# Attention phase: TensorE multiplies weights into an unused bank while it would wait, at the phase's start and in its last pair

## The reference

```python
h = tokens(x)                                  # stem convolution, offsets, deformable convolution: 36 tokens of 192
h = concatenate([h, quantised_embedding(x_txt)], axis=1)          # 36 + 128 = 164 tokens an image
h = h + attention(layernorm(h))                # 12 heads of 16, window of +-64 tokens, softmax, output projection
h = h + kan(layernorm(h))                      # two spline layers, 192 -> 512 -> 192, 16 coefficients an edge
```

```python
q, k, v = (x @ W + b).reshape(B, N, H, d).transpose(0, 2, 1, 3)   # each
scores = where(abs(i - j) <= 64, einsum('bhqd,bhkd->bhqk', q, k) * SCALE, -inf)
out = einsum('bhqk,bhkd->bhqd', softmax(scores), v)
return out.transpose(0, 2, 1, 3).reshape(B, N, D) @ Wo + bo
```

## Time and profile before

| | us |
|---|---|
| median of 3 runs | 2430.45 |
| lowest, highest | 2428.31, 2439.93 |
| profiled execution, span | 2436.7 |
| TensorE multiplying (PE) in it | 2309.0 (95%) |
| VectorE busy (DVE) | 1892.6 (78%) |
| ScalarE busy (ACT) | 1407.7 (58%) |
| GpSimd busy (POOL) | 229.4 (9%) |

### The profile page before, as it was taken

The page is one execution under the profiler, slowest core; times in us unless marked ns, Lnnn a source line. Parts: engine busy times, 40 slices in busy tenths (PEclk is TensorE's granted clock), DMA queues, the critical chain, the costliest instruction groups (busy, mean ns, idle before and its releaser), DMA issues.

```text
span 2436.7 us, 49389 instructions
## 1 busy us (share of the span) xinstructions
PE 2309.0 (95%) x20297; PEld 2155.4 (88%) x20297; DVE 1892.6 (78%) x2364; ACT 1407.7 (58%) x1391; POOL 229.4 (9%) x132
## 2 busy tenths in 40 slices
PE   7699959999999969999999999989999999999999
PEld 6366848888888859999999999989999999999999
DVE  8699745666666668676676766679999999999995
ACT  5588113444444374443534435488888888888881
POOL 5422000000000003121121211000000000000000
PEclk9799967999999969999999999999999999999999
DMA  7655130111111100000000001120000000000000
GB/s 242 164 150 149 55 145 22 44 45 45 44 45 45 45 22 20 26 19 15 26 19 26 19 15 34 64 84 23 23 23 23 23 23 23 23 23 23 23 18 10
DMA packets 99328, 116.26 MB, mean 48 GB/s; under 512 B 15271, under 2 KB 90423, under 8 KB 98487
## 3 DMA queue, kind: packets, MB, share of 16 engines
q1 hardware_dynamic: 79087, 89.38, 12.2%
q10 hardware_dynamic: 16520, 14.75, 2.0%
q0 software_dynamic: 3616, 10.54, 1.7%
HBM read 83.77 MB, written 30.86 MB: 47 GB/s over the span
## 4 chain that ended last, share of the span: by engine, by line
PE 63%; issue 0%; DVE 0%
PE spline_acc L1890 26%; PE spline_acc L1863 10%; PE spline_acc L1862 9%; PE spline_acc L1864 9%; PE spline_acc L1884 5%; PE spline_acc L1886 2%; PE spline_xT L761 0%; DVE spline_f L1639 0%; DVE spline_weights_low L1622 0%; DVE spline_x L1709 0%; DVE spline_x L1712 0%
## 5 line engine op out<-in xcount | busy, mean ns | idle before, releaser
L1890 PE MATMUL spline_acc<-spline_weights,spline_f 128*128 128x192 f32 x3936 | 672.0, 328 | 0.0
L1890 PEld LDWEIGHTS spline_acc<-spline_weights,spline_f 128*128 128x128 f32 x3936 | 637.2, 190 | 0.0
L1863 PE MATMUL spline_acc<-spline_f,spline_weights_high 128*128 128x328 f32 x1536 | 482.7, 314 | 0.0
L1862 PE MATMUL spline_acc<-spline_f,spline_weights_high 128*128 128x328 f32 x1536 | 480.1, 313 | 2.5 <-DVE spline_weights_low L1622 2.5
L1864 PE MATMUL spline_acc<-spline_f,spline_weights_low 128*128 128x328 f32 x1536 | 476.5, 310 | 0.0
L1862 PEld LDWEIGHTS spline_acc<-spline_f,spline_weights_high 128*128 128x128 f32 x1536 | 290.2, 189 | 2.8 <-DVE spline_weights_low L1622 2.8
L1863 PEld LDWEIGHTS spline_acc<-spline_f,spline_weights_high 128*128 128x128 f32 x1536 | 289.3, 188 | 0.0
L1864 PEld LDWEIGHTS spline_acc<-spline_f,spline_weights_low 128*128 128x128 f32 x1536 | 288.9, 188 | 0.0
L1884 PE MATMUL spline_acc<-spline_weights_split,spline_f_high 128*128 128x384 f32 x656 | 218.2, 389 | 8.2 <-issue 8.2
L1639 DVE SCALAR_TENSOR_TENSOR spline_f<-spline_front 128x984 fp32r<-128x984 f32 x128 | 145.5, 1177 | 100.7 <-PE spline_acc L1864 95.0
L1019 DVE TENSOR_REDUCE attend_max<-scores_by_query 82x6 f32<-82x984 f32 x128 | 150.8, 1178 | 67.8 <-PE scores_by_query L1334 67.8
(11 more groups left out here) (224 smaller groups left out, 4286.6 us busy)
## 6 DMA issues: line engine op xcount, KB each, us to landing
spline_front<-pos_scr SPq DMA_DIRECT2D x32, 540.0 KB, 4.4
hid_scr<-spline_hid SPq DMA_DIRECT2D x64, 164.0 KB, 1.8
spline_xn<-hid_scr SPq DMA_DIRECT2D x41, 256.0 KB, 3.1
attend_spread<-rec_scr SPq DMA_DIRECT2D x128, 61.5 KB, 2.2
pix_scr<-spline_front SPq DMA_DIRECT2D x32, 225.0 KB
spline_weights_raw<-w SPq DMA_DIRECT2D x1, 6144.0 KB, 21.3
spline_weights<-w SPq DMA_DIRECT2D x4, 1536.0 KB, 6.3
spline_x<-h_scr SPq DMA_DIRECT2D x41, 96.0 KB, 1.9
```

Of the source, the lines that this page charges most:

```text
L1862: nc.tensor.matmul(z, high, x_high, start=start, stop=False)
L1863: nc.tensor.matmul(z, high, x_low, start=False, stop=False)
L1890: last = nc.tensor.matmul(z, f_rest[i][:, cols], w2[:, i, r, :], start=False, stop=stop)
```

## The change

A helper `keep_going(n, spare)` issues n multiplications of 128 columns of `wqh` (the stationary operand) with the 384 columns of `wkh`, each overwriting `spare`, which nothing reads. The output is `tp`'s first bank where no key scores are pending, and once a bank of `xb` that is claimed for the transposes which follow. It is called with

- 48 at the start of the phase, with the wait for the zeros moved behind it
- 8 between the first transposes and the wait for their being read
- 9 after each of the prelude's four rounds of scores
- 18 in the first pair's first block, ahead of the second quarter's scores
- 20 at the end of `finish`, and 28 after each of the last two output projections

186 multiplications in all, each with its weight load. They carry no semaphore.

```diff
@@ -1264,8 +1264,6 @@
 
         @block.tensor
         def _(pe):
-            pe.wait_ge(zeros_set, 5)
-
             def claim(at):
 
                 bank, c = at
@@ -1277,6 +1275,11 @@
 
                 for bank, c in at:
                     pe.wait_ge(emptied[bank], c + 1)
+
+            def keep_going(n, spare):
+
+                for _ in range(n):
+                    nc.tensor.matmul(spare, wqh[:, 0, 0:P], wkh[:, 0, :], start=True, stop=True)
 
             def turn_x(t, i, at):
                 d, rows = ((0, D0), (D0, D1))[i]
@@ -1402,6 +1405,7 @@
                 for c in range(2):
                     mix(a, u, 1, c, use(t, MIX_LAST[1]))
                 project_out(a - 2, 1, use(t, Y_LAST[1]))
+                keep_going(20, tp[:, 0, 0:HG * P])
 
             def pair(tt, u, first=False, more=True):
                 t = 2 * tt + u
@@ -1419,6 +1423,8 @@
                             keys_scores(a, u, i, q // 2, most, first and i == 0)
                         if q == 0 and i == 1 and more:
                             read(use(t, K_[1]), use(t, K_[2]))
+                        if first and q == 1 and i == 0:
+                            keep_going(18, xb[:, claim(use(t, X[0])), 0:HG * P])
                         if nxt:
                             queries_scores(a + 1, w, 1 - i, q)
                         if q == 0 and not first:
@@ -1452,8 +1458,11 @@
                         for g in range(HG):
                             project(wkh, wkl, g, use(t, K_[g]))
 
+            keep_going(48, tp[:, 0, 0:HG * P])
+            pe.wait_ge(zeros_set, 5)
             for j in range(2):
                 turn_x(0, j, start(START["X"][j]))
+            keep_going(8, tp[:, 0, 0:HG * P])
             read(*(start(START["X"][j]) for j in range(2)))
             for g in range(HG):
                 project(wqh, wql, g, start(START["Q"][g]))
@@ -1464,6 +1473,7 @@
             read(start(START["K"][1]), start(START["K"][2]))
             for q in range(4):
                 queries_scores(0, 0, 0, q, True)
+                keep_going(9, tp[:, 0, 0:HG * P])
             turn_max(0, start(START["MAX"]))
             pe.wait_ge(wo_in, 16)
             pair(0, 0, first=True)
@@ -1475,6 +1485,7 @@
             pair(PAIRS // 2 - 1, 1, more=False)
             for i in range(2):
                 project_out(2 * PAIRS - 2 + i, i, use(PAIRS, Y[i]))
+                keep_going(28, tp[:, 0, 0:HG * P])
 
 
 def spline_phase(nc, front, a, h_scr, hid_scr, out, w_raw, w1_in):
```

## The result

The changed kernel takes 2432.23 us (median of 20 runs), the kernel before 2440.21 (20 runs). The ratio is 0.9969, 95% interval 0.9955 to 0.9983: 7.6 us faster (4.1 to 11.0), a real gain but under the 0.5% at which the prediction split its chances. The forecast was 12.2 us faster, 2418.3 us, in a range of 2412 to 2427; the measured time lies 13.9 us above the one and 5.2 us above the other. Most of that is the base: three runs of the kernel before gave 2430.45, twenty gave 2440.21, which is 9.8 us. The rest is the gain. Single runs of either kernel spread over more than 20 us.

The account below looks back on a forecast made before the run. TensorE, busiest and partly at half clock, was taken to bound the kernel. Start 2.3, rounds 1.0, first block 8.7, second 0.2 and end 0 sum to 12.2 us: 2418.3 us from a 2430.45 median, range 2412 to 2427.

Parts of the forecast that it names:

- What bounds it, and what the low clock costs: TensorE bounds the kernel; an added multiplication costs 0.178 us at the high clock and 0.32 us at the low one.
- The 48: Start of the phase: 11.3 us of multiplications, hidden under the first rows' layer norm; 3.2 us cost if the clock stayed low.
- The prelude: First transposes to first key scores: 2.3 us gained by transposes and projections at the high clock, 1.0 us by the rounds.
- The rounds of 9: Prelude's four score rounds: 2.63 us each with the filling, 0.3 us longer than the wait; 1.0 us gained against those measured.
- The first block: First pair: 19.9 us for 28.7 with the clock high throughout, 8.7 us gained; 1.5 us left empty behind the 18.
- the case that the clock falls there: Rival: clock falls in the first block at the 1.5 us left empty; 5.6 us gained in all, 2424.8 us; chance 0.26.
- The second block: First pair, nothing put in: starts at the high clock and loses it a little later than before; 0.2 us gained.
- the bound of 5.0: Upper bound of the second block's gain, 18.2 - 13.3 us; as a rival that the clock holds there, 2413.5 us, chance 0.13.
- The end: Last pair's 20, 28 and 28: no gain, since the phase ends with VectorE's value chain; bounds +1.5 and -2 us.
- the lower bound: The -2 us bound on the end's effect; a high clock shortens the last projection by some 2 us.
- The base: Kernel before taken at a median of 2430.45 us, three runs with a spread of 11.6, one profiled execution of 2436.7.
- The rule that was set against the change: Clock falls only after one long idle gap, so filling between rounds protects nothing: 1.2 us cost against the start's 2.3.

Follow-up runs that it names:

- hold_front2: The same kernel as hold_front, run once more for a second trace and sample of times: 0.9933 of the kernel before, 2429.68 us.
- hold_pre60: hold_front with 60 multiplications in place of 48 at the start of the phase: 0.9936 of the kernel before, 2431.51 us.
- fill28: The changed kernel with 28 multiplications in place of 18 in the first pair's first block: 0.9952 of the kernel before, 2431.74 us.
- before_look: The kernel before, unchanged, run once more for a second trace: 2430.84 us in one run.
- tail_only: The kernel before with only the 20 and 28 + 28 multiplications at attention's end: 1.0019 of the kernel before, 2449.22 us.
- hold_front: fill28 with 12 more multiplications in the first pair's second block, ahead of its second query scores: 0.9924 of the kernel before, 2421.93 us.
- front_only: The changed kernel without the 20 and 28 + 28 multiplications at attention's end: 0.9979 of the kernel before, 2443.27 us.
- hold_all: hold_pre60 with the waits of the last pair filled by multiplications too: 0.9935 of the kernel before, 2427.88 us.
- hold_thin: hold_all with 6 multiplications in place of 9 in the prelude's four rounds: 0.9915 of the kernel before, 2415.15 us.
- hold_light: hold_front with every added multiplication on 32 rows by 82 columns of weights, not 128 by 128: 1.0018 of the kernel before, 2450.0 us.

## Why the prediction was wrong, point by point

- **What bounds it, and what the low clock costs.** Right. The multiplications cost 0.173 us at the high clock, from start to start (forecast 0.178), and 0.32 at the low one, as forecast.
- **The 48.** Hidden, as forecast. What was missed is what they leave: they end 2.1 us before the transposes, and the clock fell 1.4 us behind these. I had them end 0.9 us before the transposes, by taking 6.1 us for the clock to rise; it rose after 3.5, and the gap grew. hold_front2, where it rose after 5.9 and the gap was 0.95 us, kept the clock.
- **The prelude, 3.3 us forecast, 1.9 measured.** Of the 1.4 us missing 1.0 is this fall: hold_pre60 and hold_front2, without it, give 21.7 us against 24.6, so 2.9. The rest is the rounds.
- **The rounds of 9.** 2.75 us for 2.63 forecast, without a wait and at 1.00, right but for 0.1 us each.
- **The first block, 8.7 us forecast, 2.0 measured.** This is the step that failed: that the clock would hold through this block, over the 1.5 us left empty behind the 18. The size was right and its condition was not: with 28 in place of 18 (fill28) the block is 20.1 us, forecast 19.9 (28.7 - 19.9 is 8.8; the 8.7 of the sum is a slip of 0.1). The hole of 1.5 us behind the 18 was seen and computed (1.49 measured), and the case that the clock falls there was priced at 2.3 us of gain in this block (2.0 measured) but given half the chance of the other. The trace already spoke for it: the clock had been lost beside waits of 1.27 and of 2 us, with the same light work around them. I gave too much weight to the 18 ahead of the hole: 3.4 us of full-size work did not carry the clock over the 1.5 us and the light work behind them, in three traces. The 28.7 us were also taken from one trace. The old start gave 28.7, 24.5 and 28.4 us, 27.2 on the mean, against which the changed kernel's 26.7 is a gain of 0.5.
- **The second block, 0.2 forecast, 0.8 measured**, with the fall where it was expected. The 0.8 can't be put down to the change: before_look and tail_only, with the old start, have 17.5 us too. hold_front bears out the bound of 5.0 (5.3).
- **The end, 0 forecast.** Right by front_only and tail_only, and by the reason given: the last residual follows VectorE's chain. The 2 us of the lower bound exist, but elsewhere. VectorE's norm chain waits for the projection that closes the last pair, and the change's 20 come after it. Here is that wait in the changed kernel, then the same projection in hold_pre60, where it ran at the high clock (2.18 us for 3.86):

```profile
864.00 0.55 DVE L1071 TENSOR_TENSOR attend_h<-attend_spare,attend_resid 82x384 f32<-82x384 f32 x1 [8.44 <-PE attend_spare L1394]
```

```profile
856.08 2.18 PE L1394 MATMUL attend_spare<-attend_wo,attend_oT 128*82 128x192 f32 x12 [0.70 <-ACT attend_mixed L1185]
```

  The stretch behind it is 31.3 us there, and again in hold_all and hold_thin, for 33.1 or more in every trace where it began at the low clock or the clock fell under it.
- **The base.** One profile and three times of the kernel before were taken for it. The three times were 9.8 us below the median of twenty; with the right base the forecast would have been 2428.0 us, 4.2 below the measured one. Its first block alone varies by 4.2 us (before_look) and its last pair by 4.3 (26.8 and 22.5), neither by anything in the code. Of the 7.6 us measured, the start explains 66.8 us against 71.5, 66.8 and 70.7 in three executions with the old start, 2.9 us on the mean. Of these 2.0 are the prelude, the one step that is shorter in every trace (22.7 or 22.8 for 24.6 to 24.9). 2.9 is below the interval's 4.1, and three traces are too few to say where the rest lies.
- **The rule that was set against the change.** The Trainium skill (TensorE: Matmul & The Clock Gate, section "HAM oscillation — how this bites in real kernels") ties a fall to one long idle gap. All three falls of the changed kernel stand beside gaps of 1.49 to 2.11 us, shorter than it names, and filling them removed all three (hold_pre60, fill28, hold_front). The traces disagree with it, as the forecast held; the forecast then let a 1.5 us gap pass. By that rule the prelude would have gained the start's 2.3 us less the rounds' 1.2, so 1.1; it gained 1.9, with a fall in it.

## What to carry to other kernels

Filling TensorE's waits works here as a closed chain: the waits of over 1 us beside light work are filled until dense work of the kernel itself takes over, and one hole of 1.5 us gave back 6.6 us that the fillings ahead of it had prepared. Shorter waits were borne: the pairs from the second to the last but one keep the clock with waits of up to 0.85 us in them, and 0.95 us did no harm in hold_front2. Fill with full-size operands and size each filling just under the wait (6 in place of 9 kept the clock and saved 1.3 us), and read in the trace which projection the end really follows before filling there. Where a kernel's clock is lost and regained, compare step times over several traces: one profile's step may lie 4 us from the next one's. And take the base from as many runs as the result will be measured with: here three runs missed it by more than the change gained.

## What the runs showed of the hardware that was not expected

- 48 multiplications of 32 rows by 82 columns kept TensorE busy for 15.6 us and did not raise the clock; 48 or 60 of 128 by 128 had it up 3.2 to 5.9 us after the first, in ten traces. In this phase being busy was not enough.
- TensorE busy all the time with light work can lose the clock (hold_light, at 365.8) or keep it (its second block).
- The same waits at the same place can lose it in one execution and not in the next: the last pair took 22.5 us in four and 26.1 to 27.1 us in seven of the eleven traces that leave its waits open. A fall behind a wait of 1 to 2 us is a matter of chance there; filling the wait takes the chance away.
- Ahead of attention, where nothing was changed, the same code brings the first transposes anywhere from 323.6 to 344.3 us (hold_light left out). In stretches from 51 to 116 us, first of the changed kernel and then of hold_thin, the granted clock was 0.71 and 0.82:

```profile
51.00:116.00 65.00, 32.42 (x188) 15.99 (x189) 37.72 (x59) 22.50 (x36) 42.78 (x35) 0.71 0.66 183
```

```profile
51.00:116.00 65.00, 44.87 (x237) 24.50 (x237) 49.20 (x64) 33.85 (x52) 35.62 (x28) 0.82 0.71 194
```

  The first had its transposes at 336.7, the second at 323.6. In all 13 traces the two go together: between 45 and 120 us the clock was at 0.50 for 23.9 to 44.4 us, and the start of the transposes less this time is 298.4 to 302.7 us. Which causes which is open. A multiplication takes 0.32 us at the low clock for 0.173 at the high one, so 20.5 us more at the low clock explain some 9 us of the 20.7 (an estimate from these figures); by it something else delays these phases too, and the low clock may be in part its consequence. The spread of 20.7 us is as large as that of the 20 times of the kernel before (20.8), and larger than any single step studied here.
- The spline layers, from their first multiplication to the end, took 1540.1 to 1544.9 us in kernels that don't change them. The difference lies in the second layer, which takes 832.0 to 832.6 us in seven of these traces and 835.4 to 835.9 in the other six. The kernel before has both, 832.5 in its first trace and 835.7 in before_look. The cause stays open.
